# One score piece of two PSUM banks in place of two pieces of one bank, in a four-stage transformer kernel with fixed engine orders

## What is computed

```python
x = x + tanh(g_xattn[0]) * L0_xattn(layernorm(x), ctx, ctx)   # 16 heads of 8, softmax over 1601 keys
x = x + tanh(g_ffn[0])   * L0_ffn(layernorm(x))               # top 2 of 8 experts, gelu, 128-512-128
x = x + tanh(g_xattn[1]) * L1_xattn(layernorm(x), ctx, ctx)   # softmax over the 32 greatest of 1601 scores
x = x + tanh(g_ffn[1])   * L1_ffn(layernorm(x))               # self-attention over 256 rows + top 2 of 8 experts
```

## Time and profile before

| | |
|---|---|
| median of 3 runs | 5451.87 us (5446.61 to 5455.07) |
| the profiled execution | 5462.37 us, span 5460.3 us |
| granted TensorE clock, mean | 0.936 |
| PE, DVE, ACT busy | 4684.1, 4361.7, 4036.6 us |
| first-scan matmuls (L594), 2048 | 666.3 us busy, 220.9 us idle before them |
| first-scan maxima (L1028), 2048 | 1122.3 us busy, 395.4 us idle before them |

### The profile page before, as it was taken

How to read it: one execution, slowest core, us unless ns; L and a number is a source line. 1 busy time by engine, 2 the same in 40 slices (tenths; PEclk the granted TensorE clock), 3 DMA queues, 4 the chain that set the end, 5 groups by cost and what they waited for, 6 DMA issues and landing times. The chain is left out here.

```text
span 5460.3 us, 110204 instructions
## 1 busy us (share of the span) xinstructions
PE 4684.1 (86%) x34502; PEld 2229.0 (41%) x34502; DVE 4361.7 (80%) x23240; ACT 4036.6 (74%) x5196; POOL 1154.4 (21%) x2648
## 2 busy tenths in 40 slices
PE   4878788999798889979989999997999799988776
PEld 2434334353343435334343544434353344434222
DVE  4458888878878797897879888788878888887772
ACT  1457677878687697868869788886878688787763
POOL 2121122222122222212212222222222122121110
PEclk7889899999899899989989999998999899999886
DMA  4232222223122132322313222231323223121110
GB/s 119 69 73 54 59 62 54 70 59 80 49 62 72 43 80 57 76 54 62 75 38 80 55 73 71 62 74 47 74 60 77 52 60 71 36 65 30 34 26 19
DMA packets 356337, 332.23 MB, mean 61 GB/s; under 512 B 102074, under 2 KB 313149, under 8 KB 355711
## 3 DMA queue, kind: packets, MB, share of 16 engines
q1 hardware_dynamic: 355710, 324.84, 24.3%
HBM read 217.54 MB, written 107.13 MB: 59 GB/s over the span
## 5 line engine op out<-in xcount | busy, mean ns | idle before, releaser
L942 DVE MAX8 cand<-s 128x8 f32<-128x67 f32 (+1 forms) x12288 | 1988.3, 222 | 116.8 <-ACT s L894 67.5
L913 ACT ACTIVATE prob<-wide 128x1024 f32<-128x1024 f32 (+1 forms) x1792 | 1778.7, 1025 | 390.2 <-PE wide L635 188.8
L1028 DVE TENSOR_REDUCE part<-score 128x1 f32<-128x512 f32 (+1 forms) x2048 | 1122.3, 564 | 395.4 <-PE score L594 264.1
L681 PE MATMUL att<-prob,v 128*9 128x256 f32 (+1 forms) x14336 | 1110.3, 389 | 27.9 <-ACT prob L913 26.1
L635 PE MATMUL wide<-q,k_att 128*128 128x256 bf16 (+1 forms) x6656 | 1023.4, 281 | 103.9 <-ACT s L894 56.2
L894 ACT ACTIVATE s<-wide 128x1024 f32<-128x1024 f32 (+1 forms) x1024 | 843.1, 845 | 309.6 <-DVEq L1082 174.5
L903 ACT ACTIVATE below<-wide 128x1024 bf16<-128x1024 f32 (+1 forms) x832 | 828.2, 1024 | 131.6 <-PE wide L635 123.5
L594 PE MATMUL score<-k_scan,q 128*128 128x512 bf16 (+1 forms) x2048 | 666.3, 349 | 220.9 <-DVE part L1028 178.7
L635 PEld LDWEIGHTS wide<-q,k_att 128*128 128x128 bf16 (+1 forms) x6656 | 583.3, 101 | 562.5 <-ACT s L894 149.5
L1271 POOL TENSOR_SCALAR flag<-cand,ends 128x24 bf16<-128x24 f32 x512 | 178.6, 349 | 2494.4 <-DVE ends L967 2243.5
L657 PE MATMUL wide<-below,minus_ident 128*128 128x512 bf16 (+1 forms) x1664 | 504.5, 386 | 97.2 <-ACT below L903 86.2
(11 more groups left out here) (161 smaller groups left out, 5202.2 us busy)
## 6 DMA issues: line engine op xcount, KB each, us to landing
k_scan<-k_stack SPq DMA_DIRECT2D x512, 150.1 KB, 2.6
k_stack<-split_b SPq DMA_DIRECT2D x576, 128.0 KB, 2.4
k_att<-k_stack SPq DMA_DIRECT2D x384, 192.0 KB, 3.3
ctxT<-in_ctx_dram SPq DMA_DIRECT2D x32, 800.5 KB, 5.2
q_stack<-split_b SPq DMA_DIRECT2D x192, 64.0 KB, 2.1
q<-q_stack SPq DMA_DIRECT2D x128, 96.0 KB
self_stack<-split_b SPq DMA_DIRECT2D x192, 64.0 KB, 2.1
k_self<-self_stack SPq DMA_DIRECT2D x64, 96.0 KB
```

Of the source, the lines that this page charges most:

```text
L681: r = tensor.matmul(att[32 * j:32 * j + HD + 1, 0:S], v[0:kc, c, j0 * HG + j, :], m.prob[n % 3][0:kc, j * S:(j + 1) * S], start=(c == 0), ...
L913: scalar.activation(pr[0:kc, :], ps[0:kc, :], ACT.Exp, scale=SCALE).then_inc(sem["wide_done"], 1)
L942: i = vector.max(cand[:, :, c], s[:, KCUT[c]:KCUT[c + 1]])
L1028: vector.tensor_reduce(m.part[:, QT * hh + qt, c:c + 1], score[i % 2][:, 0:wd], AX.X, ALU.max).then_inc(sem["score_max"], 1)
```

## The change

The two one-bank buffers become one tensor of two banks. The keys of a tile are cut into two pieces, 1024 columns (two matmuls, one in each bank) and 577 columns (two matmuls, 512 and 65), each with one reduction. A batch then has 64 `n0` steps and 16 z scores, 80 in all; the matmuls are the same ones. Step i waits for reduction i - 1. A z score uses the first bank and is a step of its own as before. `part` has two columns a tile. All five orders and their lags are new texts: the count of each word in a round is unchanged but for `n0` and `n0_max` (128 to 64 each). Of the orders only some lines are shown; no other function changes.

```diff
@@ ORDER @@
     pe="""
-        cut_add c1 pv.1 n0 c1 pv.1 c1 row_turn.0 c1 s_1 n0 s_1 n0 cut_add n0 cut_add w_k.1 pv.1 s_1*2 pv.1 n0*2
-        cut_add n0 cut_add s_1 pv.1 flag s_1 pv.1 cut_add n0 cut_add n0 c1 pv.1 c1 pv.1 c1 n0 c1 n0 s_1 s_0 n0 cut_add
...
+        s_1 pv.1 s_1 flag pv.1 cut_add*2 row_turn.0 c1 pv.1 c1 pv.1 c1 n0 c1 s_1 n0 s_1 cut_add*2 w_k.1 pv.1 s_1*2
+        flag pv.1 n0 cut_add*2 c1 pv.1 n0 c1 pv.1 s_1 n0 s_1 cut_add*2 c1 pv.1 n0 c1 pv.1 s_1 s_0 n0 cut_add flag pv.1
...
+        pv.1 s_1 v_w2 s_1 cut_add z_score flag cut_add z_score v_w2 c1*2 pv.1*2 s_1 row_turn.2 c1 n0 cut_add
+        row_turn.1 n0 v_w1*2 pv.1 n0 c1 v_w2 w_v.0 s_0 n0 s_0 v_w2 s_0 c1 pv.0 flag pv.0 s_0 pv.0 u_turn.1 s_0 c1 pv.0
...
     dve="""
-        rank n0_max rank n0_all rank n0_max*2 rank n0_max rank n0_max rank n0_max rank n0_max rank n0_max rank check
-        n0_max rank n0_max rank n0_max rank n0_max rank n0_max rank n0_max rank n0_max rank o_norm.1 n0_max rank check
-        n0_max least rank n0_max rank n0_max rank n0_max x_add.1 rank ln_stats.z n0_max ln_aggr.z rank ln_scale.z
...
+        rank check n0_all rank n0_max ln_stats.w rank n0_max rank*2 n0_max rank*3 check n0_max rank n0_max rank*2
+        n0_max rank*2 n0_max rank*2 n0_max check rank least o_norm.1 rank*2 n0_max rank n0_max rank x_add.1 rank*4
+        check n0_max rank*2 n0_max rank n0_max rank n0_max rank o_norm.0 n0_max rank*3 x_add.0 rank check n0_max rank
...
@@ LAG @@
-        "cut_add": 216, "c1": 244, "pv.1": 217, "n0": 255, "row_turn.0": 9, "s_1": 215, "w_k.1": 9, "flag": 62,
...
+        "s_1": 217, "pv.1": 219, "flag": 63, "cut_add": 217, "row_turn.0": 9, "c1": 244, "n0": 127, "w_k.1": 9,
...
-        "rank": 491, "n0_max": 257, "n0_all": 9, "check": 62, "o_norm.1": 17, "least": 16, "x_add.1": 5,
...
+        "rank": 490, "check": 63, "n0_all": 9, "n0_max": 128, "ln_stats.w": 1, "least": 16, "o_norm.1": 17,
...
@@ -250,7 +243,7 @@
         for name in ("row_turn", "row_minus", "shift", "rows_out", "rows_in", "u_turn", "o_norm", "att_copy"):
             of(f"{name}.{l}", name, [(l, g) for g in groups])
     for name in ("n0", "n0_max"):
-        of(name, name, [(g, hh, n) for g in groups for hh in range(HG) for n in range(8)])
+        of(name, name, [(g, hh, n) for g in groups for hh in range(HG) for n in range(4)])
     for name in ("c1", "c1_out"):
         of(name, name, [(g, n, c) for g in groups for n in range(QT * HG) for c in range(2)])
     of("rank", "rank", [(n, part) for n in range(QT * HG * NG + 1) for part in range(4)])
@@ -402,7 +395,7 @@
         m.ends = [sb(f"ends{n}", [P, HG * QT, 2, 8]) for n in range(2)]
         m.flag = sb("flag", [P, QT, KC + 1], BF16)
         m.many, m.size, m.th = sb("many", [1, 1], I32), sb("size", [P, HG * QT]), sb("th", [P, HG * QT])
-        m.part = sb("part", [P, HG * QT, 4])
+        m.part = sb("part", [P, HG * QT, 2])
         m.mx = [sb("mx0", [P, HG * QT]), m.th, sb("mx2", [P, HG * QT])]
         minus, res, shift = sb("minus", [72, P]), sb("res", [72, P]), sb("shift", [72, 3, P], BF16)
         m.minus, m.res = ([x[32 * l:32 * l + 8, :] for l in range(3)] for x in (minus, res))
@@ -424,7 +417,7 @@
         m.xnT["u"] = m.xnT["v"]
 
         wide = [psum(f"wide{n}", 2 * BANK) for n in range(2)]
-        score = [psum(f"score{n}", BANK) for n in range(2)]
+        score = psum("score", 2 * BANK)
         att, small = psum("att", BANK), psum("small", BANK)
 
         d.k_stack = [dram(f"k_stack{l}", (B, NT, HD, H, NK), BF16) for l in range(2)]
@@ -587,13 +580,15 @@
                             kn = HG * g + hh
                             q.wait_ge(k_scan_in[0][kn % 2], 16 * (kn // 2 + 1))
                             q.wait_ge(q_in[0][g % QBUF[0]], 32 * (g // QBUF[0]) + 16)
-                        if i >= 2:
-                            q.wait_ge(sem["score_max"], i - 1)
-                        qt, c = divmod(n, 4)
-                        a0, wd = c * BANK, min(BANK, NK - c * BANK)
-                        tensor.matmul(score[i % 2][:, 0:wd], m.q[0][g % QBUF[0]][:, hh, qt * P:(qt + 1) * P],
-                                      m.k_scan[0][(HG * g + hh) % 2][:, a0:a0 + wd],
-                                      start=True, stop=True).then_inc(sem["score_full"], 1)
+                        if i:
+                            q.wait_ge(sem["score_max"], i)
+                        qt, c = divmod(n, 2)
+                        a0, wd = c * 2 * BANK, min(2 * BANK, NK - c * 2 * BANK)
+                        for x in range(0, wd, BANK):
+                            n0, n1 = x, min(x + BANK, wd)
+                            r = tensor.matmul(score[:, n0:n1], m.q[0][g % QBUF[0]][:, hh, qt * P:(qt + 1) * P],
+                                              m.k_scan[0][(HG * g + hh) % 2][:, a0 + n0:a0 + n1], start=True, stop=True)
+                        r.then_inc(sem["score_full"], 1)
 
                     elif name == "c1":
                         g, n, c = key
@@ -762,10 +757,10 @@
                         i = turn("score", name, *key)
                         if h == 0:
                             q.wait_ge(kq_in[g % 2], 48 * (g // 2) + 32)
-                        if i >= 2:
-                            q.wait_ge(sem["score_max"], i - 1)
+                        if i:
+                            q.wait_ge(sem["score_max"], i)
                         for t in range(QT):
-                            r = tensor.matmul(score[i % 2][:, t * S:(t + 1) * S], q_self[0:ROWS, h, t * P:(t + 1) * P],
+                            r = tensor.matmul(score[:, t * S:(t + 1) * S], q_self[0:ROWS, h, t * P:(t + 1) * P],
                                               k_self[0:ROWS, h, :], start=True, stop=True)
                         r.then_inc(sem["score_full"], 1)
 
@@ -1019,18 +1014,18 @@
 
                     elif name == "n0_max":
                         g, hh, n = key
-                        qt, c = divmod(n, 4)
+                        qt, c = divmod(n, 2)
                         i = turn("score_out", name, *key)
                         q.wait_ge(sem["score_full"], i + 1)
                         if g and hh == 0 and n == 0:
                             q.wait_ge(sem["n0_ready"], after("n0_all", g - 1))
-                        wd = min(BANK, NK - c * BANK)
-                        vector.tensor_reduce(m.part[:, QT * hh + qt, c:c + 1], score[i % 2][:, 0:wd], AX.X,
+                        wd = min(2 * BANK, NK - c * 2 * BANK)
+                        vector.tensor_reduce(m.part[:, QT * hh + qt, c:c + 1], score[:, 0:wd], AX.X,
                                              ALU.max).then_inc(sem["score_max"], 1)
 
                     elif name == "n0_all":
                         g, = key
-                        q.wait_ge(sem["score_max"], after("n0_max", g, HG - 1, 7))
+                        q.wait_ge(sem["score_max"], after("n0_max", g, HG - 1, 2 * QT - 1))
                         if g:
                             q.wait_ge(sem["small_full"], after("row_turn", 0, g - 1))
                         vector.tensor_reduce(m.mx[0][:, :], m.part[:, :, :], AX.X, ALU.max).then_inc(sem["n0_ready"], 1)
@@ -1042,7 +1037,7 @@
                         if g and h == 0:
                             q.wait_ge(sem["small_full"], after("row_turn", 2, g - 1))
                         vector.tensor_reduce(m.mx[2][:, h * QT:(h + 1) * QT],
-                                             score[i % 2][:, :].rearrange("p (q s) -> p q s", q=QT), AX.X,
+                                             score[:, 0:BANK].rearrange("p (q s) -> p q s", q=QT), AX.X,
                                              ALU.max).then_inc(sem["score_max"], 1)
 
                     elif name == "rank":
@@ -1372,7 +1367,7 @@
                             for k in range(4):
                                 q.wait_ge(*stored("w_k", (l, b, k)))
                         if kn >= 2 and l == 0:
-                            q.wait_ge(sem["score_full"], after("n0", (kn - 2) // HG, (kn - 2) % HG, 7))
+                            q.wait_ge(sem["score_full"], after("n0", (kn - 2) // HG, (kn - 2) % HG, 2 * QT - 1))
                         elif kn >= 2:
                             q.wait_ge(sem["wide_full"], after("c1", (kn - 2) // HG, (kn - 2) % HG * QT + 1, 1))
                         sync.dma_start(m.k_scan[l][kn % 2][0:ROWS, :], d.k_stack[l][b, :, :, kn % H, :]
```

More of the change, by code:

```diff
@@ L91 @@
-        v_w2 s_0 n0*2 w_k.0 pv.0 s_0 c1 v_w2 s_0 c1 pv.0*2 n0 s_0 pv.0 s_0 n0 z_score v_w1*2 pv.0*2 flag n0 z_score
-        s_0 v_w2 w_q n0 s_0 pv.0 s_z v_w2 s_z c1 pv.0 z_score n0 s_1*2 pv_z*2 cut_add u_turn.0 cut_add z_score n0 c1
-        pv.1 w_v.0 s_1 pv.1 s_1 u_turn.2 cut_add n0*2 cut_add row_turn.2 n0 c1 pv.1 n0 c1 pv.1 s_1 ln_turn.u s_1 n0*2
-        cut_add row_turn.0 n0 cut_add z_score c1 pv.1 w_k.0 c1 pv.1 n0 s_1 z_score s_1 flag cut_add n0 cut_add z_score
-        u_q pv.1 c1 s_1 pv.1 n0 z_score s_1 cut_add n0*2 row_turn.2 cut_add c1 pv.1 n0 w_v.0 s_1 pv.1 s_1 n0*2
```

(23 more changed lines are left out.)

133 lines of the change are left out of this document (55 added, 78 removed), and 6 rows, old and new, of the table sp.

## The result

The changed kernel takes **5579.34 us** (median of 4 runs, 5575.40 to 5583.11) beside 5452.16 for the kernel before (4 runs): ratio 1.0236, 95% interval 1.0224 to 1.0248. It is 127 us slower. The forecast was 5472 and the range ended at 5535: right in sign, wrong in size.

A forecast was written before the change was run, and what follows sets the result against it. PE was taken as nearest to a bound, busy 279 of 300 us, with DVE slack. Terms -19 + 18 + 21 + 0 = +20 us on the profiled 5462.4 gave 5482, adjusted to the median as 5472; range 5408 to 5535.

The forecast's parts named there:

- Part 1, the reductions: DVE's first-scan maxima: fewer, longer reductions free 61 us by starts, 147 by durations; -19 us at the end, bounds -38 and 0.
- Part 2, the fill: Before the first n0_all: PE's write and DVE's read no longer overlap, 3.9 us a tile for 2.8; +18 us, bounds 9 and 33.
- Part 2, full rounds: Full rounds: the single score buffer makes PE wait at tight places; +1.4 us a batch, +21 us, bounds 5 and 90.
- Mechanism D: Rival, full rounds: PE stands 0.3 us at 18 to 20 tight places a batch; 90 us plus 18 in fill, 5555; chance 0.12.
- the sign that the prediction set: Clean 300 us stretch: PE's waits for reductions above 2.5 us a batch; at or below, part 2 is wrong.
- Part 3, the orders: All five engines' orders dealt anew: no sign which way; cost 0, bounds -3 and +3 us a batch, 45 us either way.
- the condition set for this: PE's waits for ACT: if they move by more than 3 us a batch, part 3 is wrong.
- PE's clock stays: Full rounds: PE's clock unchanged, since the clean stretch has 21 us of idle and 1.00; no cost charged.
- What stays, the tail: The drain after 4861 us, where no first scan runs and PE is busy 242 of 300 us: 0, within 5 us.
- short places: Full rounds: places with less PE work between score steps than DVE needs, 6 of 144 before, 18 of 80 after.

The follow-up runs named there:

- e10: The kernel before with 42 columns left out of each 512-column reduction, orders and handover alone; 5436.23 us, ratio 0.9970.
- e6: The kernel before with the keys cut 401, 400, 400, 400 in place of 512, 512, 512, 65; 5421.58 us, ratio 0.9955.
- e2: The kernel after with its new orders, but old pieces and two one-bank buffers, each n0 and n0_max doubled; 5538.60 us, ratio 1.0162 to before.
- e3: The kernel before with one single-bank score buffer instead of two, three flags moved; 6487.19 us, ratio 1.1906.
- e7: The kernel before with 8 columns in every first-scan piece, all steps and waits kept; 5325.33 us, ratio 0.9775.
- e11: The kernel after with its wide pieces cut evenly, 801 and 800 columns for 1024 and 577; 5567.71 us, ratio 1.0220 to before.
- e4: The kernel after with consecutive z scores in alternate halves of the two-bank buffer; 5587.58 us, ratio 1.0259 to before.
- e1: The kernel after, its wide pieces and single buffer under the orders of before, each second n0 and n0_max struck out, one flag moved; 5652.76 us, ratio 1.0373 to before.
- e5: The kernel before, old pieces and two buffers, with its n0 steps moved into adjacent pairs on PE and DVE; 5573.07 us, ratio 1.0233.
- e8: e2 with 8 columns in every first-scan piece; 5406.87 us, ratio 0.9912 to before.
- e9: e2 with one n0 of a pair put back between neighbouring cut_adds in 9 places, on PE alone; 5549.05 us, ratio 1.0189 to before.

## Why the prediction was right or wrong

- **Part 1, the reductions: right.** 1216 and 749 ns for 1220 and 750 forecast. The slope is (1216 - 749) / 447 = 1.04 ns, the intercept 146 ns by durations, as before. Recorded durations, added up, fell by 149 us (1154.7 to 1006.0) for 147 forecast, and DVE's busy time by 55, near the 61 of the reading by starts. What reached the end was forecast as -19 and is -16 by e10, from nearly the same 4 us a batch on the orders of before; that it was the freed time and not the shorter reduction is not shown, so the agreement may be luck. The Trainium skill's 125 ns of engine-busy time per operation on PSUM (Perfetto Trace Analysis, Optimizing Scalar/DVE Operations) would have freed 128 us; the traces show less than half. The Trainium skill's figure is of busy time, so the 60 ns by starts are what answers to it, and not the intercept of durations to which the prediction held it. The same section of the Trainium skill says that, where an engine isn't saturated but holds up others, breaking instructions up "may allow work to be completed sooner". No run here made more instructions; e6 is the nearest, with the longest reductions down from 681 to 563 ns, and it gained.
- **Part 2, the fill: right.** Forecast +18 (9 to 33), seen +20.9, and +21.7 from e2 to after. The tile of 3.9 us was exact. The first `n0_all` came at 92.0 for the 88 forecast, since the first scan itself began 4.9 us later (61.99 for 57.09): it waited for q's load, as PE's row above shows. That late start isn't what the fill lost: e2 starts its scan as late (61.3) and has no longer fill. The rule of rotating PSUM banks (the Trainium skill, Perfetto Trace Analysis, Matmuls) holds in the fill (3.9 us a tile for 2.8) and in e3 (+1040 us).
- **Part 2, full rounds: about right, as a net.** Part 1 and this part together were to give -19 + 21 = +2 in the rounds; from e2 to after the rounds change by +6.0. If e10's relief holds under the new orders too, which was not run, the handover by itself is some 20 us; this is an estimate, and the +6.0 it starts from is within the spread of the runs. Mechanism D did not decide: in the clean round PE waits 1.1 us before the pieces and 1.6 before the z scores, 2.7 for 2.5 before, and between 3100 and 3700 us it is 1.1 a batch (1.6 and 0.6 in two). By the sign that the prediction set, PE waits above 2.5 us a batch, this part isn't borne out: the +21 doesn't show as longer waits for reductions over before. The sign was a poor one, since the orders changed these waits as well.
- **Part 3, the orders: wrong, and this is the step that failed.** "I see no sign which way; cost 0, bounds -3 and +3 us a batch". e2 against before: +88 us by the ratio (+79 to +98), about 5 us a batch in the rounds, beyond the bound of 45. Of the 121 us in the profiled executions, for 20 forecast, the rounds make +83 for +2, and this term is 77 of them. The profile after meets the condition set for this: PE's waits for ACT before `c1` and `cut_add` moved by 6.4 us in a clean round. The slack was counted where the words changed in number (the score steps) and not where they changed in place. The order texts could have warned me, since PE's steps that fill the wide pair for ACT stand in other company: before, the last third of a round has them more often in blocks like `s s s s` and `c1 c1 c1 c1`, after more often in twos. That this is the cause is argued, not shown. The prediction also held that PE's clock stays: the mean granted clock fell from 0.936 to 0.929, and PE's instructions took 34 us longer.
- **What stays, the tail: mis-sized.** Forecast 0 within 5, seen +17.0: 8.9 with the orders (e2), 8.1 with piece and buffer. The kernels with the orders of before and two buffers spread from 448.4 (e7) to 457.9 (e10), and e11, which has the orders and the handover of after, has 462.4; so the size is uncertain by several us. The drain has no first scan, but it has z scores, and they hand over through the same buffer: 0.7 us of waiting each at the end, some 6 us over the last sixteen, of which e4 got back 5. The other 10 or so arise ahead of them, and no run says why.
- **A rival's sum.** D's 90 us plus 18 in the fill make 5452 + 108 = 5560, not 5555. Nothing hangs on it.

The two halves don't add in a fixed way. By way of e2 it is +88 for the orders and +41 for piece and buffer; by way of e1, +205 for piece and buffer under the old orders, and then **-73** for dealing them anew. Both come to 127 within 5 us, as near as the runs of before in each set allow. The prediction counted short places in each kernel's own orders, so its steps are those of the first way; on the second, the new orders are a repair and fall short.

"The orders" themselves hold two things, since e2 has its score steps in pairs. By way of e5 it is +123 for pairing the steps among the old words, **-34** for the new words (5573.07 to 5538.60), and +41 for piece and buffer. So full-length pairs among the old words cost more than the whole change of orders, and the new words give some of it back; with 8 columns (e7 to e8) pairs and new words together still cost 82. What the pairs alone cost with 8 columns was not run, and the loss can't be given to the new words by themselves.

**Where in the round.** The same sections of a round, cut at words that both orders have. The middle section goes from the addition of v to the fifth copy of w_k, the last third from there. First before: middle section, last third; then after: the middle section of two rounds, and the last third of the second.

```profile
3156.00:3268.00 112.00, 102.87 (x837) 41.76 (x829) 101.78 (x574) 101.56 (x128) 27.76 (x68) 1.00 0.30 72
3268.00:3389.00 121.00, 110.50 (x841) 49.57 (x841) 108.12 (x613) 99.85 (x125) 28.68 (x66) 1.00 0.29 71
```

```profile
3213.00:3330.00 117.00, 105.89 (x834) 41.95 (x828) 102.07 (x552) 101.72 (x128) 28.98 (x71) 0.97 0.28 69
3523.00:3637.00 114.00, 102.77 (x831) 41.17 (x823) 101.44 (x551) 101.36 (x128) 28.99 (x71) 1.00 0.29 71
3637.00:3762.00 125.00, 112.65 (x842) 50.09 (x840) 113.67 (x637) 99.30 (x125) 29.35 (x65) 0.99 0.27 69
```

The middle section loses 2 us at full clock and 5 with the clock at 0.97, the last third 4 (with the clock at 0.99). What stays open is which words of it do this, and on which engine, as e2 exchanged the orders of all five at once: e9 excluded the one candidate that I could name, and no run moved the others one by one. Nor was it tried whether another dealing under the wide piece would do better.

## What to carry to other kernels

Where orders are written out for each engine, a new order is not a free companion of an edit: price it as the largest unknown, with a bound from the spread of such orders and not from a share of the idle time, and run it alone under the old code. A one-deep handover has no price of its own; it costs what the number and the places of its users make it cost (here +41 and +205 us with the wide piece, 80 handovers a batch, and +1040 with 144), so count those places in the order that will run, and look at each stage that shares the buffer, the drain too. Moving steps into pairs is a change of order like any other, and cost 123 us here with nothing else changed but one flag. Before making pieces longer, try them equal: that was a small edit and gained 0.45% here (interval 0.31 to 0.59).
